# A gated cross-attention and routed-FFN kernel on one core: another order of loading, scaling and splitting the weights at its start

## Chip, cores and metric

The kernel runs on one core of one Trainium2 chip, as one launch. Its time is the device time of that core in microseconds (us). The engines have their own instruction streams: TensorE (PE in the profile, PEld for its weight loads), VectorE (DVE), ScalarE (ACT), GpSimd (POOL) and SyncE (SP), which issues the DMAs here. They are ordered among each other by semaphores alone.

## The reference, cut to what matters

```python
x = x + tanh(g_xattn[0]) * xattn(ctx_1024, layernorm(x), ...)   # x 32x112x256, ctx 32x375x256
x = x + tanh(g_ffn[0])   * routed_ffn(layernorm(x), ...)        # 8 experts, best 2 per token

def xattn(x, latents, ln_m_g, ln_m_b, ln_l_g, ln_l_b, Wq, Wkv, Wout):   # 16 heads of 64
    x, lat = layer_norm(x, ln_m_g, ln_m_b), layer_norm(latents, ln_l_g, ln_l_b)
    q, kv = lat @ Wq, concatenate([x, lat], axis=1) @ Wkv       # Wq 256x1024, Wkv 256x2048
    k, v = split(kv, 2, axis=-1)
    out = softmax(q k^T * 64 ** -0.5) v                         # per head, 112 x 487
    return out @ Wout                                           # Wout 1024x256
```

Inputs and outputs are float32.

## The kernel before, in words

Two parts follow each other: the attention for all 32 batches, and then the routed FFN with its own tiles. Only the first is touched by the change.

**Numbers in two halves.** Each float32 operand of a projection is scaled by a power of two and split into a high and a low float16 half. ScalarE writes the high half (a copy with a scale), and VectorE the low half (scaled operand minus high half, a scalar_tensor_tensor with two inputs in SBUF) for the weights, GpSimd for the normalised inputs (kv_lo, L306). Each product takes three matmuls (`three`, L622): high by high, high by low, low by high.

**Scales.** The power of two comes from the largest magnitude. `weight_scales` (L441) measures five peaks per partition on VectorE (wkv, wq, wout, and two of the layer norms' scales and shifts), TensorE turns them, VectorE takes the maxima, TensorE spreads them over the partitions, and VectorE makes exponents, scales and the factors `undo` that take the scales back. These are one chain for all four scales. `then` (L435) lets VectorE wait for each of its own small steps.

**Steps.** Work on (batch b, pair of heads j) has the step t = 8 b + j. STEPS (L39) runs from t = -24. All engines walk through the same steps, each with its own list. At step t the K and V projections of t + 8 are made (so batch 0's are in steps -8 to -1), the scores of pairs t and t + 1 on even t from t = 0 on, the product with V four steps later. The normalised input of a batch is turned (T, two units of four transposes, at j = 2 and 4, L711), scaled by the layer norm's factors on VectorE (kv_f, L538), and split; Q is made in two units at j = 3 and 7 (L719). The K, V, T and Q units use the two PSUM banks `proj_ps` in turn, and a unit waits until the one before the last has been taken out (`take`, L609): K by k_hi on ScalarE (L401) and k_lo on VectorE (L522), V by L415 and L528, T by L538 and L539, Q by L388 and L513.

**The opening.** SP issues load(0) (context and x of batch 0, L192), wkv in two halves, four small loads of the layer norms' vectors straight into their turned places (L201), tanh's and the gate's, wq, wout, load(1). The float32 weights are staged in the space of v_sb. ScalarE waits for all small loads, makes the tanh, waits for the scales and splits all of wkv (L356), then wq and wout ahead of step -9 (L379, L380). VectorE runs the statistics of batch 0, `weight_scales` at t = -22, the statistics of batch 1, the two kv_f of batch 0, the low half of wkv at t = -11, of wq at t = -6, of wout at t = -2. GpSimd subtracts the means and multiplies by the factors, and makes kv_lo of the first half at j = 4, the subtraction of the next batch at j = 5 and kv_lo of the second half at j = 6. It clears the unused rows of v_sb at t = -9 and t = -1, after the staged weights have been read. TensorE's first K of batch 0 waits for both kv_lo and for wkv's low half (L650 to L652).

## Time and profile before

| | us |
|---|---|
| median of 3 runs | 1881.23 (1879.61 to 1881.39) |
| profiled execution | 1880.83 |
| its span | 1879.1 |
| TensorE busy | 1657.4 (88% of the span) |
| VectorE busy | 1348.8 (72%) |
| ScalarE busy | 1186.2 (63%) |
| GpSimd busy | 1185.2 (63%) |
| DMA | 233.20 MB, mean 124 GB/s |

The span is the time from the first to the last recorded instruction of one execution; the device time holds a little more around it. An engine's busy time is the sum of its instructions; its share of the span is an average over stages with different limits. In a timeline each row is an instruction (or several merged, with their count): start, duration, engine, line, operation, what is written and read, shape, and in brackets how long the engine had been idle before it and what released it.

### The profile page before, as it was taken

How to read it: one execution, taken by the hardware profiler on the slowest of the kernel's cores; microseconds unless marked ns; L12 is line 12 of the kernel's file. 1: busy time of each engine (PE TensorE's matmuls, PEld its weight loads, DVE VectorE, ACT ScalarE, POOL GpSimd, SP SyncE). 2: the span in 40 equal slices, each digit the busy share in tenths (PEclk: the TensorE clock that was granted, in tenths of full speed). 3: DMA queues.
4: the chain of work that ended last, by engine and by line, in shares of the span. 5: the costliest groups of instructions: out<-in, count | busy, mean ns of one | idle time of the engine just before them, and what ended most of it. 6: DMA issues, size and time to landing. Idle time of an engine off the chain costs nothing. (4 is left out here: it accounts for less than half of the span.)

```text
span 1879.1 us, 42970 instructions
## 1 busy us (share of the span) xinstructions
PE 1657.4 (88%) x15031; PEld 1161.6 (62%) x15032; DVE 1348.8 (72%) x3173; ACT 1186.2 (63%) x2666; POOL 1185.2 (63%) x1297
## 2 busy tenths in 40 slices
PE   2899999999999999999999999997303999999980
PEld 0456666666666666666666666665202999989970
DVE  5777877778777787777877778775495666666646
ACT  2587887778877787777877778776244333333320
POOL 4477778777787777877778777767163433434420
PEclk9999999999999999999999999998556999999995
DMA  4267767667777776666766667667454111111119
GB/s 132 50 132 143 152 138 139 138 142 152 138 138 138 142 153 138 136 140 142 154 138 137 139 142 142 129 128 151 124 178 154 51 45 50 47 47 50 45 36 292
DMA packets 599543, 233.20 MB, mean 124 GB/s; under 512 B 534064, under 2 KB 584016, under 8 KB 598992
## 3 DMA queue, kind: packets, MB, share of 16 engines
q1 hardware_dynamic: 592656, 212.67, 52.7%
q0 software_dynamic: 6720, 18.36, 3.2%
q8 instruction: 98, 1.61, 0.3%
q14 instruction: 69, 0.57, 0.1%
HBM read 78.66 MB, written 20.19 MB: 53 GB/s over the span
## 5 line engine op out<-in xcount | busy, mean ns | idle before, releaser
L279 POOL TENSOR_TENSOR p_parts<-p_f,p_parts 112x487 f16<-112x487 f32 x512 | 559.6, 1116 | 185.6 <-ACT p_parts L373 185.6
L364 ACT ACTIVATE p_f<-scores_ps,shift 112x487 f32<-112x487 f32 x512 | 337.7, 664 | 7.9 <-DVE passed L494 4.2
L494 DVE TENSOR_SCALAR_CACHE_REDUCE passed<-scores_ps 112x487 f16<-112x487 f32 x512 | 308.0, 658 | 30.2 <-PE scores_ps L645 30.2
L401 ACT ACTIVATE k_hi<-proj_ps 128x488 fp32r<-128x488 f32 x256 | 148.0, 578 | 256.1 <-PE proj_ps L627 256.0
L1010 ACT ACTIVATE space<-h_ps,b_sb,undo 128x256 f32<-128x256 f32 x280 | 142.6, 559 | 233.4 <-PE h_ps L1239 231.0
L528 DVE SCALAR_TENSOR_TENSOR v_sb<-proj_ps,v_sb 128x512 f16<-128x512 f32 (+1 forms) x256 | 176.9, 691 | 140.6 <-ACT v_sb L415 139.4
L373 ACT ACTIVATE p_parts<-p_f 112x487 f16<-112x487 f32 x512 | 275.8, 607 | 0.0
L522 DVE TENSOR_TENSOR k_lo<-proj_ps,k_hi 128x488 fp32r<-128x488 f32 x256 | 169.0, 660 | 91.4 <-ACT k_hi L401 91.2
L676 PE MATMUL pv_ps<-v_sb,pt_sb 128*128 128x128 f16 x2048 | 218.2, 221 | 7.6 <-DMA pt_sb<-p_parts 4.8
L627 PE MATMUL proj_ps<-kv_hi,wkv_hi 128*128 128x488 f16 x512 | 191.4, 374 | 28.7 <-POOL kv_lo L306 13.5
L627 PE MATMUL proj_ps<-wkv_hi,kv_hi 128*128 128x512 f16 (+1 forms) x512 | 194.3, 379 | 0.3
L627 PE MATMUL proj_ps<-wkv_lo,kv_hi 128*128 128x512 f16 (+1 forms) x512 | 194.1, 379 | 0.0
L627 PE MATMUL proj_ps<-wkv_hi,kv_lo 128*128 128x512 f16 (+1 forms) x512 | 194.0, 379 | 0.0
L627 PE MATMUL proj_ps<-kv_hi,wkv_lo 128*128 128x488 f16 x512 | 189.4, 370 | 0.0
L627 PE MATMUL proj_ps<-kv_lo,wkv_hi 128*128 128x488 f16 x512 | 189.4, 370 | 0.0
L1262 PE MATMUL y_ps<-w_hi,stage 128*128 x1120 | 189.0, 273 | 0.0
L981 POOL DMA_INDIRECT y_rows<-space,y_row_i x70 | 69.4, 991 | 147.7 <-DVE space L1179 137.0
L415 ACT ACTIVATE v_sb<-proj_ps 128x512 f16<-128x512 f32 (+1 forms) x256 | 152.8, 597 | 14.5 <-PE proj_ps L627 5.6
L1239 PE MATMUL h_ps<-xt_hi,w_hi 128*128 128x256 f16 x560 | 154.6, 276 | 5.0 <-DVE xt_lo L1171 5.0
L676 PEld LDWEIGHTS pv_ps<-v_sb,pt_sb 128*128 128x128 f16 x2048 | 134.7, 99 | 37.2 <-DMA pt_sb<-p_parts 5.5
L1239 PE MATMUL h_ps<-xt_hi,w_lo 128*128 128x256 f16 x560 | 154.6, 276 | 0.0
L1239 PE MATMUL h_ps<-xt_lo,w_hi 128*128 128x256 f16 x560 | 154.6, 276 | 0.0
(222 smaller groups left out, 4017.1 us busy)
## 6 DMA issues: line engine op xcount, KB each, us to landing
w_part<-in_L_ffn_w_dram SPq DMA_DIRECT2D x64, 256.0 KB, 3.5
stage<-in_L_ffn_w_dram SPq DMA_DIRECT2D x32, 512.0 KB, 4.5
ctx_sb<-in_ctx_dram SPq DMA_DIRECT2D x32, 375.0 KB
space<-y_rows SPq DMA_DIRECT2D x32, 224.0 KB, 4.7
pt_sb<-p_parts SPq DMA_TRANSPOSE x256, 4.0
x_sb<-in_x_dram SPq DMA_DIRECT2D x32, 112.0 KB
res_sb<-in_x_dram SPq DMA_DIRECT2D x32, 112.0 KB, 5.3
x_dram<-x_sb SPq DMA_DIRECT2D x32, 112.0 KB, 2.9
```

The lines of the kernel that those rows point to most:

```text
L279: pool.tensor_tensor(p_parts[0:LQ, p % PS, h, 1, 0:LK], p_f[0:LQ, p % 2, h, 0:LK], p_parts[0:LQ, p % PS, h, 0, 0:LK], ALU.subtract).then_i ...
L364: act.activation(p_f[0:LQ, p % 2, h, 0:LK], scores_ps[n][0:LQ, 0:LK], ACT.Exp, bias=shift[0:LQ, p // 2 % 2, n:n + 1], scale=-1.0, accum_ou ...
L373: act.activation(p_parts[0:LQ, p % PS, h, 0, 0:LK], p_f[0:LQ, p % 2, h, 0:LK], ACT.Copy).then_inc(p_high, 1)
L401: act.activation(k_hi[:, j], ps[:, 0:LKP], ACT.Copy).then_inc(kq_high, 1)
L415: act.activation(v_sb[0:rows, (b + 1) % 2, c, 8 * half_:8 * half_ + 8, 0], ps[0:rows, :].rearrange("p (n d) -> p n d", d=DH), ACT.Copy, sc ...
L494: dve.tensor_scalar(passed[0:LQ, n], scores_ps[n][0:LQ, 0:LK], P_SHIFT, None, ALU.add, ALU.min, accum_out=shift[0:LQ, p // 2 % 2, n:n + 1] ...
L522: dve.tensor_tensor(k_lo[:, j], ps[:, 0:LKP], k_hi[:, j].bitcast(F32), ALU.subtract).then_inc(kq_low, 1)
L528: dve.scalar_tensor_tensor(out=v_of(1), in0=ps[0:rows, :].rearrange("p (n d) -> p n d", d=DH), scalar=V_SCALE, in1=v_of(0), op0=ALU.mult, ...
L627: last = nc.tensor.matmul(out, lhs(a, k), rhs(c, k), start=(n == 0), stop=(n == 3 * KD - 1))
L676: last = nc.tensor.matmul(pv_ps[:, at:at + 128], block_of(0, c), v_sb[:, sv, c, n].rearrange("p a d -> p (a d)"), start=(c == 0), stop=(c ...
L1239: last = nc.tensor.matmul(h_ps[m][:, c * ROWS:c * ROWS + ROWS], (w1_hi, w1_lo)[a][:, k, bass.ds(e1, 1), f:f + 128].rearrange("p o f -> p ( ...
L1262: last = nc.tensor.matmul(y_ps[s][:, r * D:r * D + D], (g_hi, g_lo)[a][:, s, m, c, r * 128:r * 128 + 128], (w2_hi, w2_lo)[b][:, m * 2 + c, ...
```

## The change

It concerns the opening up to step 1 of the attention.

- The layer norms' four vectors are loaded as rows, two of 128 values each, into `ln_rows`, ahead of load(0), and TensorE turns all eight rows at once into `tail_ps`; VectorE copies them to `affine`.
- wkv is loaded in four chunks of 512 columns (first K, first V, second K, second V), each with its own semaphore. The tanh's and the gate's loads stand behind load(1).
- There are four chains of scales in place of one: for the inputs (turn 0), wkv (1), wq (2), wout (3). wkv is measured chunk by chunk. wq is measured behind wkv's first two low halves and its scale is made at t = -6; wout is measured at t = -4 and its scale made at t = -2.
- The weights are split in seven parts: kv0 and kv1 ahead of the first projection, kv2, q0, kv3, q1 between steps -8 and -3, out at t = -1 (high) and t = 0 (low). TensorE waits for the parts one by one.
- wkv is staged in p_parts and wout in pt_sb; wq stays in v_sb. So v_sb's first half is cleared at the start, and p_parts' and pt_sb's unused columns at t = -1 and t = 1. ScalarE's step 0 waits for p_parts, and the first transpose of p on SP for wout's low half.
- GpSimd makes both kv_lo of batch 0 at j = 4.

```diff
+            for n, a in enumerate((ln_m_g, ln_m_b, ln_l_g, ln_l_b)):
+                sp.dma_start(ln_rows[KD * n:KD * (n + 1), :], a.rearrange("(k p) -> k p", p=128)).then_inc(small_loaded, 16)
             load(0)
-            for k in range(KD):
-                sp.dma_start(stage[:, k], wkv[k * 128:(k + 1) * 128]).then_inc(w_loaded, 16)
-            for n, a in enumerate((ln_m_g, ln_m_b, ln_l_g, ln_l_b)):
-                sp.dma_start(affine[:, n, :], a.rearrange("(k p) -> p k", p=128), allow_slow_non_contiguous=True).then_inc(small_loaded, 16)
-            sp.dma_start(tanh_g[:, :], g_x.partition_broadcast(128)).then_inc(small_loaded, 16)
-            sp.dma_start(gate_sb[:, :, :], gate_w.rearrange("(k p) e -> p k e", p=128)).then_inc(small_loaded, 16)
+            for n in range(4):
+                sp.dma_start(kv_chunk(stage, n), kv_chunk(wkv.rearrange("(k p) n -> p k n", p=128), n)).then_inc(w_loaded[n], 16)
...
             load(1)
+            sp.dma_start(tanh_g[:, :], g_x.partition_broadcast(128)).then_inc(tanh_loaded, 16)
+            sp.dma_start(gate_sb[:, :, :], gate_w.rearrange("(k p) e -> p k e", p=128)).then_inc(gate_loaded, 16)
...
-                if j in (4, 6) and is_batch(nb):
-                    k = (j - 4) // 2
+                halves = ((0, 1) if j == 4 else ()) if nb == 0 else ((j - 4) // 2,) if j in (4, 6) and is_batch(nb) else ()
+                for k in halves:
...
+                if t == -2 * NP + 2:
+                    weight_high("kv0")
+                    weight_high("kv1")
+                if t == -NP - 1:
+                    act.wait_ge(tanh_loaded, 16)
+                    act.activation(tanh_g[:, :], tanh_g[:, :], ACT.Tanh).then_inc(tanh_done, 1)
                 if t == 0:
-                    act.wait_ge(set_up, 2)
+                    act.wait_ge(parts_cleared, PS)
...
+                for turn, at in (("kv2", -8), ("q0", -6), ("kv3", -6), ("q1", -4), ("out", -1)):
+                    if t == at:
+                        weight_high(turn)
...
+            def input_scale():
+                largest(0, 3, 5)
+                power(0, 3, 5)
+                then(dve.tensor_scalar(affine[:, :, :].rearrange("p a k -> p (a k)"), affine[:, :, :].rearrange("p a k -> p (a k)"), scale[:, 3:4], None, ALU.mult))
+
+            def kv_scale():
+                for n in range(4):
+                    dve.wait_ge(w_loaded[n], 16)
+                    last = dve.tensor_reduce(peak_kv[:, n:n + 1], kv_chunk(stage, n), AX.XY, ALU.max, apply_absolute_value=True)
+                then(last)
+                then(dve.tensor_reduce(peak[:, 0:1], peak_kv[:, :], AX.X, ALU.max))
+                dve.sem_inc(peaks_moved, 1)
+                largest(1, 0, 1)
+                power(1, 0, 1)
+                dve.sem_inc(scales_ready, 1)
...
+                if t == -3 * NP:
+                    input_peaks()
                 if t == -3 * NP + 2:
-                    weight_scales()
+                    input_scale()
+                    kv_scale()
                 if t == -NP - 3:
-                    split_kv_weights()
-                if t == -NP + 2:
-                    split_q_weights()
-                if t == -2:
-                    split_out_weights()
+                    weight_low("kv0")
+                    weight_low("kv1")
+                    q_peak()
...
+                for turn, at in (("kv2", -7), ("q0", -5), ("kv3", -5), ("q1", -3), ("out", 0)):
+                    if t == at:
+                        weight_low(turn)
+                if t == -8:
+                    largest(2, 1, 2)
+                if t == -6:
+                    q_scale()
+                if t == -4:
+                    out_peak()
+                if t == -3:
+                    largest(3, 2, 3)
+                if t == -2:
+                    out_scale()
```

On ScalarE and VectorE the parts stand behind the V evacuation of their step (L415, L528), and on VectorE ahead of the T evacuation of the same step. TensorE turns and spreads the peaks of wq behind V at t = -8 and -7, those of wout at t = -3 and -2.

## Rows read from the trace of the kernel before

**Rows 1.** Stretches: bounds, length, busy time of each engine, granted clock, DMA, GB/s.
```profile
40.00:72.00 32.00, 27.13 (x154) 12.69 (x156) 19.01 (x31) 11.14 (x20) 15.35 (x13) 1.00 0.17 48
72.00:86.00 14.00, 12.80 (x71) 6.08 (x68) 11.60 (x33) 10.53 (x25) 5.62 (x7) 1.00 0.18 33
...
200.00:300.00 100.00, 99.07 (x910) 63.97 (x908) 76.87 (x203) 77.98 (x185) 77.33 (x89) 1.00 0.69 138
...
1100.00:1200.00 100.00, 99.07 (x909) 63.87 (x908) 76.48 (x198) 77.34 (x184) 78.05 (x89) 1.00 0.68 133
```

**Rows 2.** TensorE's timeline: the first K and the first V projection.
```profile
40.05 0.59 PE L627 MATMUL proj_ps<-kv_hi,wkv_hi 128*128 128x488 f16 x1 [13.47 <-POOL kv_lo L306]
...
42.46 0.59 PE L627 MATMUL proj_ps<-wkv_hi,kv_hi 128*128 128x512 f16 x1
```

**Rows 3.** SP's timeline: issue of one small load.
```profile
5.15 0.47 SPq L201 DMA_DIRECT2D affine<-in_L_xattn_ln_l_b_dram  x1
```

**Rows 4.** VectorE's timeline up to the low half of wkv.
```profile
7.43 1.08 DVE L546 BATCH_NORM_STATS2 stats<-ctx_sb 125x6 f32<-125x256 f32 x3 [7.29 <-DMA x_sb<-in_x_dram]
...
14.12 4.41 DVE L448 TENSOR_REDUCE att_peak<-v_sb 128x1 f32<-128x4096 f32 x1
...
20.64 2.28 DVE L452 TENSOR_REDUCE att_peak<-v_sb 128x1 f32<-128x2048 f32 x1
23.53 0.28 DVE L455 TENSOR_REDUCE att_peak_t<-tail_ps 5x1 f32<-5x128 f32 x1 [0.61 <-PE tail_ps L605]
...
24.80 0.16 DVE L459 COPY att_peak_e<-tail_ps 128x5 f32<-128x5 f32 x1 [0.73 <-PE tail_ps L607]
...
26.33 0.23 DVE L469 TENSOR_SCALAR affine<-affine,att_scale_i 128x8 f32<-128x8 f32 x1
...
27.89 1.08 DVE L546 BATCH_NORM_STATS2 stats<-ctx_sb 125x6 f32<-125x256 f32 x3
...
29.63 0.64 DVE L538 TENSOR_SCALAR kv_f<-proj_ps,affine 128x375 f32<-128x375 f32 x1
...
31.36 4.60 DVE L481 SCALAR_TENSOR_TENSOR wkv_lo<-v_sb,att_scale_i,wkv_hi 128x2048 f16<-128x2048 f32 x2
```

**Rows 5.** ScalarE's timeline: the high half of wkv.
```profile
26.27 3.89 ACT L356 ACTIVATE wkv_hi<-v_sb,att_scale_i 128x2048 f16<-128x2048 f32 x2 [12.08 <-DVEq L468]
```

**Rows 6.** GpSimd's timeline: kv_lo and the subtraction between its halves.
```profile
31.40 5.53 POOL L306 TENSOR_TENSOR kv_lo<-kv_f,kv_hi 128x488 f16<-128x488 f32 x1
36.89 1.46 POOL L328 TENSOR_TENSOR norm_sb<-ctx_sb,moments 125x768 f32<-125x768 f32 x1
...
38.89 1.10 POOL L306 TENSOR_TENSOR kv_lo<-kv_f,kv_hi 128x488 f16<-128x488 f32 x1
```

**Rows 7.** Timelines of GpSimd and VectorE near 99 us.
```profile
98.61 2.19 POOL L279 TENSOR_TENSOR p_parts<-p_f,p_parts 112x487 f16<-112x487 f32 x2 [1.22 <-ACT p_parts L373]
...
99.34 1.21 DVE L586 TENSOR_REDUCE peaks<-w_part 128x2 f32<-128x1024 f32 x1
```

**Rows 8.** Timelines of TensorE and VectorE: steps -3 and -2, and the first scores.
```profile
60.69 0.38 PE L627 MATMUL proj_ps<-kv_hi,wkv_hi 128*128 128x488 f16 x1 [0.99 <-DVE v_sb L528]
61.94 0.38 PE L627 MATMUL proj_ps<-wkv_hi,kv_hi 128*128 128x512 f16 x1
...
63.47 0.38 PE L627 MATMUL proj_ps<-kv_hi,wkv_hi 128*128 128x488 f16 x1
...
71.72 0.48 PE L645 MATMUL scores_ps<-k_hi,q_hi 64*112 64x488 f32 x2
...
62.74 0.67 DVE L522 TENSOR_TENSOR k_lo<-proj_ps,k_hi 128x488 fp32r<-128x488 f32 x1 [1.24 <-ACT k_hi L401]
64.06 0.69 DVE L528 SCALAR_TENSOR_TENSOR v_sb<-proj_ps,v_sb 128x512 f16<-128x512 f32 x1 [0.65 <-ACT v_sb L415]
64.67 2.34 DVE L489 SCALAR_TENSOR_TENSOR wout_lo<-v_sb,att_scale_i,wout_hi 128x2048 f16<-128x2048 f32 x1
```

**Rows 9.** VectorE's timeline: k_lo of step 1.
```profile
78.54 0.65 DVE L522 TENSOR_TENSOR k_lo<-proj_ps,k_hi 128x488 fp32r<-128x488 f32 x1
```

More of the change, by code:

```diff
@@ L351, in _, with weight_high @@
         def _(act):
-            act.wait_ge(small_loaded, 16 * 6)
-            act.activation(tanh_g[:, :], tanh_g[:, :], ACT.Tanh).then_inc(tanh_done, 1)
-            act.wait_ge(scales_ready, 1)
-            for k in range(KD):
-                act.activation(wkv_hi[:, k], stage[:, k], ACT.Copy, scale=scale[:, 0:1]).then_inc(w_high, 1)
+            def weight_high(turn):
+                if turn == "kv0":
+                    act.wait_ge(scales_ready, 1)
+                if turn == "q0":
+                    act.wait_ge(scales_ready, 2)
+                if turn == "out":
+                    act.wait_ge(scales_ready, 3)
+                    act.activation(wout_hi[:, :, :], stage_out, ACT.Copy, scale=scale[:, 2:3]).then_inc(w_high, 1)
+                elif turn[0] == "q":
+                    n = int(turn[1])
+                    act.activation(q_chunk(wq_hi, n), q_chunk(stage_q, n), ACT.Copy, scale=scale[:, 1:2]).then_inc(w_high, 1)
+                else:
+                    n = int(turn[2])
+                    act.activation(kv_chunk(wkv_hi, n), kv_chunk(stage, n), ACT.Copy, scale=scale[:, 0:1]).then_inc(w_high, 1)
             def exponential(p, h):
@@ L439, in then, with largest @@
                 dve.wait_ge(scale_step, n_step[0])
-            def weight_scales():
-                flat = lambda a: a.rearrange("p k n -> p (k n)")
-                dve.wait_ge(small_loaded, 16 * 6)
-                dve.tensor_reduce(peak[:, 3:4], affine[:, 0:4:2, :], AX.XY, ALU.max, apply_absolute_value=True)
-                dve.tensor_reduce(peak[:, 4:5], affine[:, 1:4:2, :], AX.XY, ALU.max, apply_absolute_value=True)
-                dve.wait_ge(w_loaded, 32)
-                dve.tensor_reduce(peak[:, 0:1], flat(stage), AX.X, ALU.max, apply_absolute_value=True)
+            def largest(turn, first, last):
+                at = slice(first, last)
+                dve.wait_ge(peaks_moved, 4 * turn + 2)
+                then(dve.tensor_reduce(peak_t[0:last - first, :], tail_ps[0:last - first, 0:128], AX.X, ALU.max))
+                then(dve.tensor_scalar(peak_diag[0:last - first, at], ident[0:last - first, 0:last - first], peak_t[0:last - first, :], None, ALU.mult))
+                dve.sem_inc(peaks_moved, 1)
@@ new lines, in power @@
+            def power(turn, first, last):
+                at = slice(first, last)
+                dve.wait_ge(peaks_moved, 4 * turn + 4)
+                then(dve.tensor_copy(peak_e[:, at], tail_ps[:, 128:128 + last - first]))
+                if turn == 0:
+                    then(dve.scalar_tensor_tensor(out=peak_e[:, 3:4], in0=peak_e[:, 3:4], scalar=16.0, in1=peak_e[:, 4:5], op0=ALU.mult, op1=ALU.add))
+                    at = slice(3, 4)
+                then(dve.tensor_scalar(exponent[:, 0, at], peak_e[:, at].bitcast(I32), 23, None, ALU.arith_shift_right))
+                then(dve.tensor_scalar(exponent[:, 1, at], exponent[:, 0, at], -1.0, 268.0, ALU.mult, ALU.add))
+                then(dve.tensor_scalar(exponent[:, 2, at], exponent[:, 1, at], 156.0, None, ALU.min))
+                then(dve.tensor_scalar(exponent[:, 3, at], exponent[:, 2, at], -1.0, 254.0, ALU.mult, ALU.add))
+                then(dve.tensor_scalar(scale_i[:, :, at], exponent[:, 2:4, at], float(2 ** 23), None, ALU.mult))
@@ L468, in weight_scales, with q_scale @@
-                dve.sem_inc(scales_ready, 1)
-                then(dve.tensor_scalar(affine[:, :, :].rearrange("p a k -> p (a k)"), affine[:, :, :].rearrange("p a k -> p (a k)"), scale[:, 3:4], None, ALU.mult))
+            def q_scale():
+                power(2, 1, 2)
                 then(dve.tensor_tensor(undo[:, 2:3], inverse[:, 3:4], inverse[:, 0:1], ALU.mult))
-                then(dve.tensor_scalar(undo[:, 3:4], undo[:, 2:3], inverse[:, 2:3], 1.0 / V_SCALE, ALU.mult, ALU.mult))
                 then(dve.tensor_scalar(undo[:, 4:5], undo[:, 2:3], inverse[:, 3:4], -float(DH) ** -0.5, ALU.mult, ALU.mult))
@@ L473, in weight_scales, with out_peak, out_scale @@
                 then(dve.tensor_scalar(undo[:, 0:1], undo[:, 4:5], inverse[:, 1:2], None, ALU.mult))
+                dve.sem_inc(scales_ready, 1)
+            def out_peak():
+                dve.wait_ge(wout_loaded, 16)
+                then(dve.tensor_reduce(peak[:, 2:3], stage_out, AX.XY, ALU.max, apply_absolute_value=True))
+                dve.sem_inc(peaks_moved, 1)
+            def out_scale():
+                power(3, 2, 3)
+                then(dve.tensor_scalar(undo[:, 3:4], undo[:, 2:3], inverse[:, 2:3], 1.0 / V_SCALE, ALU.mult, ALU.mult))
@@ L683, in _ @@
                     if ob == 0:
-                        pe.wait_ge(w_ready, 4)
+                        pe.wait_ge(w_ready, W_TURN["out"])
                     pe.wait_ge(o_moved[s], 16 * (ob // 2 + 1))
```

120 lines of the change are left out of this document (70 added, 50 removed).

## Prediction

> **What bounds the kernel now.** I read three views in this order. First the stretches of time: from 200 to 300 us TensorE is busy for 99.07 of 100 us, and again so from 1100 to 1200 [rows 1]. So the attention is paced by TensorE, and whatever TensorE has behind it when this regime begins is handed on unchanged to the end; the routed part behind it isn't touched by the change. The opening is different: from 40 to 72 us TensorE is busy 27.13 of 32 us, from 72 to 86 us 12.80 of 14 [rows 1]. Second, TensorE's timeline: the first projection starts at 40.05, after 13.47 us of waiting for GpSimd's kv_lo (L306) [rows 2]. So what the change is worth is (how much earlier the first projection starts) minus (how much longer the eight steps t = -8 to -1 and the first steps behind them take). Third, the timelines of the other engines: up to 40 us for the first term, from 40 to 86 us for the second.
>
> **Loads.** Four row loads now stand ahead of load(0). One such issue costs the SP queue 0.47 us, taken from the smallest scale-and-shift load of before [rows 3], so the first inputs are issued 1.9 us later. The statistics began at 7.43, at once when x had landed [rows 4]; I put them at 9.3. (Bounds: 0, if they land by bandwidth and not by issue, to 2.5.) wkv comes in four chunks behind them; everything else of 4 bytes a piece that stood ahead of wq is gone or behind load(1), so I cost landing at nothing: the reductions begin at 14.1 below, which is when they began before with all of wkv there [rows 4]. The tanh and gate loads go behind load(1); their readers come after t = -9 and later.
>
> **First scales.** Statistics and aggregation take 29.63 - 27.89 = 1.74 [rows 4], so to 11.1. The input scale then runs from largest to the scaled affine: 23.53 to 26.33 + 0.23 = 26.56, that is 3.0 us [rows 4]; its turning on TensorE has been done by then. 14.1. Measuring wkv: 4.41 us for 4096 columns, here in four parts [rows 4], plus 0.1 for the reduction over them: 18.7. From the end of the last peak, 20.64 + 2.28 = 22.92, to the first split on ScalarE, 26.27, passed 3.35 us [rows 4, 5]; one instruction of 0.2 less: 3.2. The scale of wkv is there at 21.9 instead of 26.2. What made before late is plain: it measured wq and wout (two times 2.28 [rows 4]) ahead of all scales, and waited for the smallest loads before it began.
>
> **First halves.** DVE: statistics of batch 1, 1.74, to 23.7; then the two affine halves, 31.36 - 29.63 = 1.73 [rows 4], to 25.4; then only the two wkv chunks that steps -8 to -5 need, 2048 of 4096 columns, half of 4.60 = 2.3 [rows 4], to 27.7. ScalarE has the two high halves (half of 3.89 [rows 5]) at 24.0 and kv_hi at 26.1, so it isn't last. GpSimd: kv_lo stretched to 5.53 while DVE ran its two-input splits and ended 0.97 after them; alone it took 1.10 [rows 6]. I take the same here: first half at 27.7 + 1.0, second at 29.9, because the change lets both go ahead of the subtraction that stood between them (38.89 - 36.89 = 2.0 [rows 6]). q_peak on DVE (2.2 us) now runs beside them; a reduction with one input did not stretch GpSimd: p_parts took 2.19 for two, 1.1 each, across the 1.21 us reduction of w_part [rows 7]. If it did stretch them, 2.2 more. The clearing of v_sb moves to GpSimd's idle time before 9 us and costs nothing. **First projection at 30.0 instead of 40.05: 10 us gained** (bounds 7 to 12).
>
> **The eight steps.** Now the price: what was done before the first projection is put into the steps behind it. A step goes like this [rows 8]: K from 60.69, through ScalarE's k_hi to DVE's k_lo 2.05 later, its bank free 0.73 on: the next K at 63.47, a step of 2.8 us, though TensorE's own work for K and V is 2.5 (K to V 1.25). V from 61.94, v_lo 2.12 later, bank free after 0.75 more. Walking the eight steps of before with these numbers, T and Q units (0.5 and 1.25 us) and its one wq split and one wout split (2.3 each) included, gives the first scores at 71.5; the trace has 71.72 [rows 8]. So the walk is good to some tenths, and DVE has only about 0.6 us free between v_lo and the next k_lo: what is put there and is longer is paid. The same walk of the new order from 30.0, with a quarter-chunk split at 1.14 on DVE and 0.97 on ScalarE (halves of the above):
> - t = -8: ScalarE kv2 high, DVE largest 0.5 (as 24.06 - 23.53 [rows 4], about), then the statistics as before: next K at 34.1, and at 38.0 behind the kv2 split of t = -7.
> - t = -6: DVE power and undo: 24.80 to 26.33 less the one that only the input needs, and three undo steps, together 1.95 us [rows 4], behind v_lo at 41.3, so to 43.9; the T evacuation (0.9) queues behind that, which holds V of t = -5 until 44.9. ScalarE stands at q0 from 41.8 to 43.9, then splits q0 and kv3, 1.9 us, and only at 45.85 takes K of t = -5, which has been ready since 43.5. Behind ScalarE wait k_lo, V's evacuation and everything of DVE.
> - t = -5: Q needs wq_lo 0, which stands on DVE behind k_lo and v_lo: 49.2. TensorE waits 3.0 us there. The next K starts at 50.5.
> - t = -4: out_peak, 2.2 us, stands ahead of the T evacuation; V of t = -3 waits for it until 57.7 (1.9 us idle).
> - t = -3 to -1: q1 split, largest, out scale (1.65 us), wout high (1.9 us on ScalarE): next K's at 59.1 and 62.8, first scores at 67.0.
>
> TensorE idles 10.9 us in these steps, against 6.1 by the same walk of before. They take 37.0 instead of 31.4 by walk: 5.5 longer. **What is left at the first scores: 71.7 - 67.0 - 0.2 for the walk's own lag = 4.5.** A page of the Trainium skill speaks against this stage: TensorE: Matmul & The Clock Gate, section HAM oscillation, says that gaps of idle TensorE can send it back to the half clock. By the rows of this trace I take nothing for it (rival C); by that page the sum could be some us worse.
>
> **The first steps of attention.** The wout split, 2.34 us on DVE [rows 8], moves from t = -2 to t = 0, between v_lo and the statistics. Before, k_lo of t = 1 started at 78.54 with no idle time in front of it [rows 9], and DVE is busy 11.60 of 14 us from 72 to 86 [rows 1]. So all 2.3 of it are late there; DVE's pauses, 14 - 11.60 = 2.4 us in that stretch, about half of them behind the split, take 1.0 back: 1.3 lost (bounds 0 to 2.3). The clearing of p_parts (GpSimd, t = -1, idle then) and the waits of the first transpose and of GpSimd at t = 1 for the wout split cost nothing: by the walk it ends near 75, before ScalarE has turned out the first high half of p.
>
> **Sum.** 10.05 - 5.55 - 1.3 = 3.2 us gained. Against the profiled execution, span 1879.1 and 1880.83 with what lies around it, 1877.6; the median of the three runs, 1881.23, is 0.4 above that execution, so I say 1878.0.
>
> **Rivals.**
> A, the inserted work is hidden. Then the steps are as long as before, 31.7, and 10.05 - 1.3 = 8.8 are gained: 1872.5. For it: TensorE has 5 us idle from 40 to 72 [rows 1]. Against it: that idle time is itself waiting for DVE, and ScalarE's wait at q0 is a new one. 0.12; half of it would do (about 1875).
> B, the beginning gains less. If load(0) lands late by 2.5, q_peak stretches GpSimd (2.2) and the wout split costs its full 2.3, the sum is 10.05 - 0.6 - 2.2 - 5.55 - 2.3 = -0.6: 1881.8. It is decided by where the first projection starts: past 33 us nothing is left. 0.25 that it goes to within 1.5 us of no change.
> C, slower. The first six matmuls of before take 2.41 us, 40.05 to 42.46 [rows 2], those of a later K 1.25, 60.69 to 61.94 [rows 8]: 0.40 and 0.21 apart, as at the lower (1.2 GHz) and the upper (2.4 GHz) level, the former after 13.5 us of idleness, though the granted clock of the stretch is printed as 1.00 [rows 1]. If the 3.0 us of idleness in front of Q at t = -5 bring the lower pace back and it stays, the 48 matmuls of four steps cost 0.2 more each, 9.6, and two Q's 1.2 each, 12 in all, of which the idle 4 us of these steps hide a third: 8 net, 3.2 - 8 = -4.8: 1885.9. The rule of the clock page named above would do this in part; the 4.9 us of short idle times of before brought no such thing by 60.69. The point from which it decides is whether matmuls behind the Q of t = -5 are 0.21 apart. 0.04.
> D, it doesn't do what it says: another late thing sets the first projection (a chunk of wkv, the norm). Each is due 2 us or more ahead by the sum, 0.05, about 1880.
>
> **How the numbers follow.** My forecast has 0.54, with a range of its own from 1876 to 1880. 0.2% of 1881 is 3.8 us, about what a measurement of this kernel can tell from no change. Of the forecast's 0.54 a little under a half, 0.25, lies below 1877.4, and A gives 0.12: faster 0.37. Slower is C and the tail of B: 0.06. The rest, 0.57, is within. The range goes from 1874.5, the half of A, to 1882, the end of B.
>
> **What would show it.** Right: scale of wkv near 22 us, kv_lo's second half ending near 30, first projection right behind; wq split 0 as what ends a TensorE wait of 2 to 3 us in front of Q; out_peak in front of an evacuation, with nearly 2 us idle; first scores near 67; the stretch from 200 us on unchanged. Wrong: kv_lo stretched past DVE's splits by q_peak; stages of half pace; a first projection past 33; or steps no longer than before.

## The result, and the profile after

The changed kernel is slower: 1883.5 us median against 1880.49 for the kernel before in the same comparison, ratio 1.0018 with a 95% interval of 1.0011 to 1.0025, that is 2 to 5 us. The profiled execution has a span of 1882.0 us (1879.1 before). I had said 1878.0, in a range of 1874.5 to 1882.0.

The stretches (bounds, length, busy time of TensorE, its weight loads, VectorE, ScalarE, GpSimd, granted clock, DMA share, GB/s) answer to [rows 1]; first those of the rows, then two short ones for the clock:

```profile
40.00:72.00 32.00, 20.84 (x107) 9.54 (x108) 22.74 (x48) 12.84 (x20) 10.05 (x14) 0.95 0.12 32
72.00:86.00 14.00, 12.51 (x84) 6.43 (x84) 11.87 (x30) 9.96 (x22) 4.38 (x5) 1.00 0.06 11
...
200.00:300.00 100.00, 99.07 (x915) 64.13 (x913) 76.38 (x197) 77.35 (x184) 78.80 (x90) 1.00 0.71 138
1100.00:1200.00 100.00, 99.07 (x913) 64.19 (x912) 76.67 (x200) 77.36 (x184) 78.95 (x90) 1.00 0.68 132
```
```profile
32.00:36.00 4.00, 4.00 (x11) 1.41 (x10) 0.67 (x1) 0.58 (x1) 3.50 (x4) 1.00 0.19 32
60.00:64.00 4.00, 2.77 (x8) 1.03 (x9) 1.54 (x3) 0.61 (x1) 2.68 (x3) 0.59 0.00 0
```

From 200 us on nothing has changed. From 40 to 72 us TensorE does a quarter less, 20.84 us against 27.13, although it began 8.5 us earlier. TensorE's timeline, the lines that answer to [rows 2] and [rows 8] (start, duration, engine, line, operation, tiles, shape, idle time before it and what ended it):

```profile
31.52 0.59 PE L711 MATMUL proj_ps<-kv_hi,wkv_hi 128*128 128x488 f16 x1 [8.46 <-POOL kv_lo L314]
...
36.71 0.44 PE L711 MATMUL proj_ps<-kv_hi,wkv_hi 128*128 128x488 f16 x1
...
47.69 0.42 PE L711 MATMUL proj_ps<-wkv_hi,kv_hi 128*104 128x512 f16 x1 [1.49 <-DVE kv_f L612]
...
52.13 0.22 PE L711 MATMUL proj_ps<-kv_hi,wq_hi 128*128 128x112 f16 x1 [2.95 <-DVE wq_lo L548]
...
61.23 0.61 PE L711 MATMUL proj_ps<-wkv_hi,kv_hi 128*128 128x512 f16 x1 [1.98 <-DVE kv_f L612]
61.63 0.64 PE L711 MATMUL proj_ps<-wkv_lo,kv_hi 128*128 128x512 f16 x1
...
63.98 0.46 PE L711 MATMUL proj_ps<-kv_hi,wkv_hi 128*128 128x488 f16 x1
...
72.02 0.21 PE L711 MATMUL proj_ps<-kv_hi,wq_hi 128*128 128x112 f16 x1 [1.49 <-DVE k_lo L582]
73.31 0.48 PE L729 MATMUL scores_ps<-k_hi,q_hi 64*112 64x488 f32 x2
```

The first projection starts 8.5 us earlier than before, the first scores 1.6 us later: the eight steps take 41.8 us instead of 31.7. The waits are those that the walk had named, with nearly its sizes: 1.49 for V at t = -5, 2.95 for wq_lo at t = -5, 1.98 for V at t = -3, behind out_peak. The 1.49 in front of Q at 72.02 (t = -1) it had not named. The matmuls at 61.23 to 63.98 are 0.4 us apart, the lower pace; the granted clock of 60 to 64 us is 0.59.

The products with V, by tile (count, shortest, median and longest duration in ns, then the starts of the first and the last), of the kernel before and of the changed one:

```profile
L676 PE MATMUL pv_ps<-v_sb,pt_sb x2048: 216/219/314, 92.8 to 1319.0; 128*128 128x128 f16 x187
```
```profile
L770 PE MATMUL pv_ps<-v_sb,pt_sb x2048: 216/219/315, 95.6 to 1320.5; 128*128 128x128 f16 x187
```

The first is 2.8 us later, about what the medians show (3.0). From the first to the last lie 1226.2 and 1224.9 us, so in these two executions the last is only 1.5 later; in all thirteen kernels of this study it is 1224.8 to 1226.2, and what follows up to the end of the span has 558.9 to 561.9 without a pattern. So a single span says nothing below 2 to 3 us here, and I read each kernel by three marks of its opening, with its median and ratio beside them. The marks come from one profiled execution of each kernel. The kernel before was measured anew beside each group of runs, and the ratio is to that: its median was 1880.49 for the changed kernel and e1 to e4, 1879.89 for e5 to e8, 1881.13 for e9 and e10, 1880.48 for e11. So kernels of different groups are better compared by their ratios.

| kernel | first projection | first scores | first product with V | median | ratio to before, 95% interval |
|---|---|---|---|---|---|
| before | 40.05 | 71.72 | 92.8 | 1880.49 | |
| changed | 31.52 | 73.31 | 95.6 | 1883.5 | 1.0018 (1.0011 to 1.0025) |
| e1_apart | 31.63 | 72.92 | 95.2 | 1882.38 | 1.0009 (1.0 to 1.0019) |
| e2_load1_first | 30.06 | 71.77 | 94.1 | 1882.06 | 1.0011 (1.0001 to 1.002) |
| e3_before_halves | 37.90 | 70.67 | 91.8 | 1877.66 | 0.9985 (0.9976 to 0.9995) |
| e4_warm | 31.80 | 71.87 | 94.2 | 1882.24 | 1.0006 (0.9997 to 1.0016) |
| e5_chain_early | 31.49 | 68.74 | 91.0 | 1878.17 | 0.9993 (0.9984 to 1.0003) |
| e7_early_load1_apart | 29.51 | 66.69 | 88.9 | 1876.02 | 0.9977 (0.9968 to 0.9987) |
| e6_all | 29.77 | 65.54 | 87.8 | 1875.6 | 0.9977 (0.9966 to 0.9988) |
| e8_before_halves_warm | 38.29 | 69.83 | 90.9 | 1877.31 | 0.9984 (0.9975 to 0.9994) |
| e9_fill_stage | 31.77 | 73.42 | 95.7 | 1881.64 | 1.0002 (0.9993 to 1.0011) |
| e10_out_earlier | 30.25 | 67.25 | 88.3 | 1875.18 | 0.9967 (0.9955 to 0.998) |
| e11_stats_later | 29.99 | 64.13 | 86.3 | 1872.53 | 0.9958 (0.9945 to 0.9972) |

Two things scatter in these marks that the edits don't explain. The last input of batch 0 landed between 8.98 and 9.71 us in e7, e6, e10 and e11, which have the same loads in the same order, and it moves all that follows. And the number of matmuls at the lower pace differs. I count the K and V matmuls recorded with 0.5 us or more instead of 0.37 to 0.46. In the eight kernels whose first units start without unused matmuls ahead of them, 7 to 14 of them open the eight steps (7 before, 14 in e3, 12 changed, 9 in e1, 7 in e2, 14 in e9, 12 in e5 and e7), and each costs 0.2 us. A difference of 1 us between two kernels can be this alone, and has to be looked for step by step.

### The profile page after: what moved, and what is told of

Same layout as the page of the kernel before. It is cut to its first block and busy times, and to the rows that moved or that the text cites. A ratio compares the mean times of both kernels' runs of the same rounds, so it can differ in the third digit from the quotient of the medians.

```text
span 1882.0 us, 43038 instructions
## 1 busy us (share of the span) xinstructions
PE 1663.0 (88%) x15041; PEld 1163.4 (62%) x15042; DVE 1356.0 (72%) x3205; ACT 1186.7 (63%) x2669; POOL 1179.2 (63%) x1297
```

## The experiments

**Two engines hold each other up.** In the changed kernel the input scale took 1.1 us more than I had given it. VectorE's timeline of the changed kernel:

```profile
12.77 0.15 DVE L488 TENSOR_SCALAR att_exponent<-att_exponent 128x1 int32<-128x1 int32 x1
12.96 1.15 DVE L489 TENSOR_SCALAR att_scale_i<-att_exponent 128x2 int32<-128x2 int32 x1
14.14 0.54 DVE L501 TENSOR_SCALAR affine<-affine,att_scale_i 128x8 f32<-128x8 f32 x1
```

GpSimd's timeline of the same stretch:

```profile
12.61 1.47 POOL L336 TENSOR_TENSOR norm_sb<-ctx_sb,moments 125x768 f32<-125x768 f32 x1
14.04 0.61 POOL L337 TENSOR_TENSOR norm_sb<-x_sb,moments 112x256 f32<-112x256 f32 x1
```

The step of 2 values a partition ends as GpSimd's subtraction does, 14.11 and 14.08; the one of 1 value at 12.77 ran through beside the same subtraction.

> The changed kernel, but GpSimd holds its subtraction for batch 0 back until the input scale is made, and its multiplication for batch 2 until the scale of wout is made. In the changed kernel one VectorE step of 0.17 us took 1.15 (12.96 to 14.11, just as GpSimd's subtraction ended at 14.08), and again 1.34 at 69.22, ending with GpSimd's multiplication at 70.53. Theory: the two engines hold each other up there. Then both steps take 0.17, the affine step 0.23 instead of 0.54, wkv's measuring begins 1.3 earlier (13.4). For the second place the first scores come 1.2 earlier relative to the first projection. Whether the first projection is earlier too is open: if the landing of batch 1's input (23.4) sets its statistics, it stays at 31.5 and the total gains 1.2 us; if not, it starts at 30.2 and the total gains 2.5. Rival: the long steps have another cause (TensorE's or a DMA's), and nothing moves.

```diff
+                    if nb == 2:
+                        pool.wait_ge(scales_ready, 3)
...
+                    if nb == 0:
+                        pool.wait_ge(input_scaled, 1)
...
+                    dve.sem_inc(input_scaled, 1)
```

VectorE's timeline of e1_apart:

```profile
13.00 0.17 DVE L493 TENSOR_SCALAR att_scale_i<-att_exponent 128x2 int32<-128x2 int32 x1
13.20 0.23 DVE L505 TENSOR_SCALAR affine<-affine,att_scale_i 128x8 f32<-128x8 f32 x1
...
23.59 1.08 DVE L624 BATCH_NORM_STATS2 stats<-ctx_sb 125x6 f32<-125x256 f32 x3 [2.34 <-DMA x_sb<-in_x_dram]
```

Both steps are short again, and so is the second place (0.17 at 70.00): the hold-up is shown. The first projection did not move; VectorE waits 2.34 us for batch 1's x in place of 1.10. So of the first hold-up nothing was lost in this kernel, load(1) hid it. From the second I had expected 1.2 us; the first scores come only 0.4 earlier. TensorE's wait in front of Q shrank from 1.49 to 0.90 and the step t = -1 from 5.49 to 4.89 us: half of the 1.2. In front of it two other stretches fell to the lower pace (matmuls 0.4 us apart from 53.12 to 55.9 and from 62.6 to 66.0, 15 in all against 6 in the changed kernel; at the first projection it has 9 of them and not 12). The Trainium skill, SBUF — State Buffer, section SBUF: two separate sides, says that VectorE and GpSimd share one pair of ports, which a GpSimd instruction, or a VectorE one in a two-port mode or (against a GpSimd one that reads SBUF) with two inputs in SBUF, holds for its whole length. The rows agree, the step of two values ending 0.03 us behind GpSimd's instruction; that the step of one value at 12.77 was not held is this trace's own.

**Batch 1's input.**

> The changed kernel with load(1) issued ahead of wq and wout. In the changed kernel VectorE stood idle 1.10 us at 22.4 until x of batch 1 had landed, ahead of the statistics that its queue has in front of kv_f. Theory: this idle time goes, the first projection starts at 30.4 instead of 31.5, and the total gains 1.1 us, all of it kept because the steps behind keep their lengths. Rival: wq or wout now land late (their measuring at 29.4 and 57.7 would wait) or GpSimd is last anyway: no gain.

```diff
+            load(1)
             sp.dma_start(stage_q, wq.rearrange("(k p) n -> p k n", p=128)).then_inc(wq_loaded, 16)
             sp.dma_start(stage_out, wout.rearrange("(j p) n -> p j n", p=128)).then_inc(wout_loaded, 16)
-            load(1)
```

VectorE's timeline, batch 1's statistics, of the changed kernel and of e2_load1_first:

```profile
23.49 1.08 DVE L619 BATCH_NORM_STATS2 stats<-ctx_sb 125x6 f32<-125x256 f32 x3 [1.10 <-DMA x_sb<-in_x_dram]
```
```profile
22.25 1.08 DVE L619 BATCH_NORM_STATS2 stats<-ctx_sb 125x6 f32<-125x256 f32 x3
```

The statistics began without a wait, the first projection at 30.06 and the first scores at 71.77, both 1.5 earlier where the theory had 1.1; batch 0's input had landed 0.26 earlier too. The eight steps keep their length, 41.7 us, but not unit by unit: 7 matmuls at the lower pace at the first projection instead of 12, and 12 later on instead of 6. The interval of the ratio (1.0001 to 1.002) can't tell the total from that of the changed kernel.

**One part of the change alone.**

> The kernel before with one part of the change alone: GpSimd makes both kv_lo of batch 0 at j = 4, ahead of the subtraction for batch 1. Theory: kv_lo's second half ends 2.0 us earlier (38.0), the first projection starts at 38.0 and the first scores at 69.7; the steps behind it stay as they are, so the total is 2.0 us lower than the kernel before. Rival: the subtraction and the clearing of v_sb now come behind and hold batch 1's turned input back by the 2 us: total unchanged.

```diff
-                if j in (4, 6) and is_batch(nb):
-                    k = (j - 4) // 2
+                halves = ((0, 1) if j == 4 else ()) if nb == 0 else ((j - 4) // 2,) if j in (4, 6) and is_batch(nb) else ()
+                for k in halves:
...
                     pool.wait_ge(kvlo_done, 2)
+                    pool.wait_ge(pool_step, subtracted(1))
```

First projection at 37.90, 2.15 earlier; first scores 1.05 and first product with V 1.0 earlier; median 2.8 below before, interval 0.9 to 4.5 us. It is a gain by itself. Half of the 2.15 went in the first steps, where the lower pace lasted longer (14 matmuls and not 7; the second K came 4.98 us behind the first, 3.98 before). The edit put nothing there, so that this half was lost to the scatter, and is not a price of the edit, is likely but not shown.

**The lower pace at the first projection.**

> The changed kernel with 22 unused matmuls of 128x512 (into PSUM that nothing reads then) on TensorE between the first wkv part and the wait for kv_lo, so that TensorE is busy from about 24 us to the first projection. Theory: the first K and V run at the upper pace, 0.21 us apart instead of 0.41 to 0.43 (5.2 us for twelve becomes 2.6), the second K starts 2.3 us earlier relative to the first, and the first scores and the total are some 2 us earlier. Rival: VectorE and ScalarE pace these steps, and the time is given back before the first scores: total unchanged. The unused matmuls may themselves push the first projection back by up to 1 us.

```diff
+                        if b == -1:
+                            pe.wait_ge(w_high, 1)
+                            for i in range(22):
+                                nc.tensor.matmul(tail_ps[:, :], wkv_hi[:, 0, 0:128], wkv_hi[:, 0, 0:512], start=True, stop=True)
                         pe.wait_ge(kvlo_done, 2 * (b + 1) + 2)
```

TensorE's timeline of e4_warm, the unused matmuls:

```profile
23.76 6.39 PE L737 MATMUL tail_ps<-wkv_hi 128*128 128x512 f16 x22 [0.64 <-ACT wkv_hi L376]
```

The second K stands 2.78 us behind the first instead of 5.19: 2.4 us, as expected. At the first scores 1.7 of them are left (40.1 behind the first projection instead of 41.8): K of t = -4 now ran at the lower pace too, beside a stretch at t = -3 and -2 as in the changed kernel. The medians, 1.3 apart, don't tell the two kernels apart.

> The kernel before with GpSimd's two kv_lo of batch 0 behind each other (alone: first projection 37.90, last product with V 2.0 us earlier) and 20 unused matmuls of 128x512 on TensorE from the end of wkv's high half to the first projection. Theory: the first K and V run at the upper pace, the first scores come another 1.5 us earlier (69.1 instead of 70.67), total some 1876. Rival: the steps are paced by VectorE and ScalarE there: total as without them, 1877.7.

In e8_before_halves_warm, which is the run e3_before_halves with 20 such matmuls, the first scores stand 31.5 us behind the first projection instead of 32.8, and come 0.84 earlier. The theory had 1.5, the rival nothing: the second V now waits 1.18 us for VectorE's v_lo, so about half is taken by VectorE. The ratios, 0.9984 and 0.9985, don't tell the two apart.

> The changed kernel with 8 unused matmuls of 128x512 on TensorE in front of the Q unit of t = -5, where it waits 2.95 us, and 8 in front of V of t = -3, where it waits 1.98. In the changed kernel V of t = -3 ran at the lower pace (2.6 us instead of 1.3) behind these waits. Theory: idleness of TensorE brought the lower pace; filled, the V of t = -3 runs at 0.21 us a matmul, no other unit falls, and the first scores come 1.0 to 1.5 us earlier relative to the first projection (from 41.8 us behind it to about 40.5); the total moves by about 1 us. Rival: the fall has nothing to do with idleness, and V of t = -3 or a unit near it is slow as before.

```diff
+                    if t == -3:
+                        for i in range(8):
+                            nc.tensor.matmul(tail_ps[:, :], wkv_hi[:, 0, 0:128], wkv_hi[:, 0, 0:512], start=True, stop=True)
...
+                    if b == -1 and n == 0:
+                        pe.wait_ge(w_high, W_TURN["q0"])
+                        for i in range(8):
+                            nc.tensor.matmul(tail_ps[:, :], wkv_hi[:, 0, 0:128], wkv_hi[:, 0, 0:512], start=True, stop=True)
```

TensorE's timeline of e9_fill_stage, the first matmul of V at t = -5:

```profile
47.92 0.60 PE L711 MATMUL proj_ps<-wkv_hi,kv_hi 128*104 128x512 f16 x1 [1.49 <-DVE kv_f L612]
```

V of t = -3 ran at the upper pace (first matmul 62.36, next K 63.77), and its step took 4.81 us instead of 6.14. But the lower pace had come at 47.9, ahead of the long wait, so it took V at t = -5 and part of the unused matmuls, and the Q unit came 0.9 us later relative to K of t = -5. First scores 41.65 us behind the first projection, as without. That no other unit would fall failed. Up to this V, TensorE's instructions are those of the changed kernel, where the same V, behind the same wait of 1.49, ran at the upper pace (0.42 at 47.69): which unit the lower pace hits is not set by the code alone. The trace is one execution; by the ratios, 1.0002 (0.9993 to 1.0011) against 1.0018 (1.0011 to 1.0025), the kernel is some 3 us below the changed one, with intervals that just touch. So that nothing was gained holds for this trace and is open for the total.

**The place of the work, not its amount.**

> The changed kernel with other places for the work on wq and wout, and the same amount of splitting: both are measured behind wkv's first low halves (VectorE is idle there from 31.6 to 34.8), one chain makes both scales in step -8, and the splits stand one to a step (high kv2 -8, q0 -7, kv3 -6, q1 -5, out -3; low kv2 -7, q0 -6, kv3 -5, q1 -3, out -1). Theory: the places cost, not the work. The waits of TensorE in front of Q at t = -5 (2.95 us), of V at t = -5 and -3 (1.49 and 1.98) and of Q at t = -1 (1.49) go, and with them the second fall to the lower pace (1.3 us for V of t = -3); first projection as before at 31.5, first scores near 66.5 instead of 73.3, the total 6 to 7 us below the changed kernel (about 1877). Rival: VectorE's work between the steps is what costs, wherever it stands (it has some 0.6 us free in a step); then the steps are at most 2 us shorter and the total is 1881 or more.

```diff
                     weight_low("kv1")
                     q_peak()
+                    out_peak()
+                if t == -8:
+                    largest(2, 1, 3)
...
-                for turn, at in (("kv2", -7), ("q0", -5), ("kv3", -5), ("q1", -3), ("out", 0)):
-                    if t == at:
-                        weight_low(turn)
...
                     dve.tensor_scalar(kv_f[:, k, LC:LK], ps[:, LC:LK], affine[:, 2, k:k + 1], affine[:, 3, k:k + 1], ALU.mult, ALU.add).then_inc(kv_affine, 1)
+                for turn, at in (("kv2", -7), ("q0", -6), ("kv3", -5), ("q1", -3), ("out", -1)):
+                    if t == at:
+                        weight_low(turn)
```

ScalarE's list changes with it:

```diff
-                for turn, at in (("kv2", -8), ("q0", -6), ("kv3", -6), ("q1", -4), ("out", -1)):
+                for turn, at in (("kv2", -8), ("q0", -7), ("kv3", -6), ("q1", -5), ("out", -3)):
```

Two things go beyond the places of the splits: VectorE's low halves now stand behind the T evacuation of their step and not ahead of it, and one chain of small steps makes what two made.

TensorE's timeline of e5_chain_early:

```profile
42.89 0.38 PE L705 MATMUL proj_ps<-kv_hi,wkv_hi 128*128 128x488 f16 x1 [2.98 <-DVE k_lo L583]
...
48.70 0.38 PE L705 MATMUL proj_ps<-kv_hi,wkv_hi 128*128 128x488 f16 x1 [1.00 <-DVE v_sb L589]
...
51.57 0.21 PE L705 MATMUL proj_ps<-kv_hi,wq_hi 128*128 128x112 f16 x1 [0.17 <-DVE k_lo L583]
...
68.74 0.48 PE L723 MATMUL scores_ps<-k_hi,q_hi 64*112 64x488 f32 x2
```

From the same first projection the first scores come 4.6 us earlier than in the changed kernel; the wait for wq_lo went from 2.95 to 0.17 and those behind the T evacuations are gone. One new wait took 2.98, for k_lo behind the chain of small steps and the statistics that now stand in step -8, and eight matmuls at the lower pace follow it. So the theory holds for two thirds of its size. The total is 5.3 us below the changed kernel by the medians, 4.7 by the ratios (0.9993 against 1.0018, intervals apart); the rival, 1881 or more, is refuted.

> The kernel of the run above, with load(1) issued ahead of wq and wout, and with GpSimd's subtraction for batch 0 held back until the input scale is made. Each alone, in the changed kernel: load(1) first moved the first projection from 31.52 to 30.06; the subtraction apart moved the scale of wkv 1.1 us forward (VectorE then waited 2.34 us for batch 1's input instead of 1.10) and left the first projection at 31.63. Theory: load(1)'s landing hid the second gain; with both the first projection is at about 29.0, first scores another 2.5 earlier than in the run above, total about 1874.5. Rival: GpSimd's kv_lo or wq's landing takes over and the first projection is at 30 or later.

First projection 29.51, first scores 66.69, 2.0 and 2.05 earlier than in e5_chain_early; the median is 2.2 lower. What e1 couldn't show alone (the early hold-up, hidden by load(1)) shows with e2's edit: the first projection is at 29.51 against 30.06, though batch 0's input landed 0.39 later (8.98 against 8.59). From that landing it is 20.5 us against 21.5: worth 0.9.

> The kernel of the run above with 18 unused matmuls of 128x512 on TensorE ahead of the first projection. In the changed kernel 22 of these brought the first K and V to the upper pace and the first scores 1.7 us nearer to the first projection. Theory: the same here, first scores 1.5 to 2.5 us earlier, total about 1873. Rival: the first steps have VectorE's chain of wq's and wout's scales beside them and are paced by it, so that nothing is gained.

TensorE's timeline of e6_all, between the first K and the first V:

```profile
32.30 0.27 PE L679 MATMUL tail_ps<-ident,att_peak 128*2 128x128 f32 x1 [1.12 <-DVEq L530]
32.41 0.38 PE L708 MATMUL proj_ps<-wkv_hi,kv_hi 128*128 128x512 f16 x1
```

The first scores are 35.8 us behind the first projection instead of 37.2, and come 1.15 earlier; the medians, 0.4 apart, don't tell them apart. Part of what the upper pace gives is taken at once: TensorE is through with the first K sooner and waits 1.12 us for wout's measuring, which VectorE has to do before the first V.

> The kernel with all of it (chains early, load(1) first, subtraction apart, unused matmuls ahead of the first projection; first scores 65.54), with wout's split one step pair earlier: high at t = -5, low at t = -4, and wq's second half high at -4, low at -3. In the kernels so far wout's low half (2.3 us of VectorE) stood at t = 0 or -1, and the first product with V came 22.3 us behind the first scores; where it stood at t = -2 it came 21.1 us behind. Theory: the 1.2 us are this split in the way of the minima; here 21.1 again, first product with V near 87, total about 1 us below 1875.6. Rival: it costs the same at t = -4, where the evacuation of T is queued behind the K and V ones: first scores 1 us later and nothing gained.

Against e6_all:

```diff
-        W_TURN = {"kv0": 1, "kv1": 2, "kv2": 3, "q0": 4, "kv3": 5, "q1": 6, "out": 7}
+        W_TURN = {"kv0": 1, "kv1": 2, "kv2": 3, "q0": 4, "kv3": 5, "out": 6, "q1": 7}
...
-                for turn, at in (("kv2", -8), ("q0", -7), ("kv3", -6), ("q1", -5), ("out", -3)):
+                for turn, at in (("kv2", -8), ("q0", -7), ("kv3", -6), ("out", -5), ("q1", -4)):
...
-                for turn, at in (("kv2", -7), ("q0", -6), ("kv3", -5), ("q1", -3), ("out", -1)):
+                for turn, at in (("kv2", -7), ("q0", -6), ("kv3", -5), ("out", -4), ("q1", -3)):
```

The first product with V is 21.1 us behind the first scores, as predicted, and the first scores 37.0 behind the first projection instead of 35.8: 58.1 against 58.0 in sum. That looks like the rival. But the steps, each from its K to the next (the last to the first scores), say where the 1.2 us are:

| step | -8 | -7 | -6 | -5 | -4 | -3 | -2 | -1 |
|---|---|---|---|---|---|---|---|---|
| e6_all | 4.38 | 5.65 | 5.70 | 5.31 | 4.12 | 2.78 | 3.68 | 4.15 |
| e10_out_earlier | 5.85 | 5.55 | 5.52 | 5.31 | 4.12 | 3.72 | 2.77 | 4.16 |
| e11_stats_later | 5.90 | 3.88 | 4.32 | 5.31 | 4.12 | 3.15 | 3.31 | 4.15 |

TensorE's timeline of e6_all and then of e10_out_earlier, the first K, a matmul of the first V, and the second K:

```profile
29.77 0.38 PE L708 MATMUL proj_ps<-kv_hi,wkv_hi 128*128 128x488 f16 x1 [0.77 <-POOL kv_lo L314]
...
32.63 0.38 PE L708 MATMUL proj_ps<-wkv_lo,kv_hi 128*128 128x512 f16 x1
...
34.15 0.38 PE L708 MATMUL proj_ps<-kv_hi,wkv_hi 128*128 128x488 f16 x1
```
```profile
30.25 0.38 PE L708 MATMUL proj_ps<-kv_hi,wkv_hi 128*128 128x488 f16 x1 [1.68 <-POOL kv_lo L314]
...
33.38 0.63 PE L708 MATMUL proj_ps<-wkv_lo,kv_hi 128*128 128x512 f16 x1
...
36.10 0.38 PE L708 MATMUL proj_ps<-kv_hi,wkv_hi 128*128 128x488 f16 x1
```

The loss is in t = -8, 1.47 us, ahead of everything that the edit moves: the first V ran at the lower pace. Where the split went, t = -3 is 0.94 longer, and t = -2, from which wout's high half has gone (in e6_all ScalarE makes it from 58.17 to 60.16), 0.91 shorter. From the second K on, e10 is 0.2 us shorter up to the first scores and 1.1 in the first steps of attention. So this trace speaks for the theory, not for the rival: the low half at t = -4, with the high half ahead of it, costs nothing net, and the low half at t = 0 or -1 costs 1.2 us. The ratios, 0.9967 and 0.9977, lean the same way and don't separate the two.

> The kernel with all of it (first scores 65.54, first product with V 87.8), with two things taken out of step -8: the statistics of batch 2 (1.3 us of VectorE) go to t = -4, and wout's last factors to t = -7. In the kernels with the early chain TensorE waits 2.9 us for k_lo in front of K of t = -6, behind a chain of small steps and these statistics, and the matmuls right after that wait run at the lower pace (eight of them, 1.7 us). Theory: the wait shrinks to 1.3 us or less, the fall to the lower pace behind it goes, and the price at t = -4 is at most 1 us: first scores 2 us earlier, 63.5, total about 1 us or more below the kernel with all of it. Rival: the lower pace comes anyway (it is not that one wait that brings it), and the statistics cost at t = -4 what they cost at t = -8: first scores within 1 us of 65.5.

```diff
                     q_scale()
+                if t == -7:
                     out_scale()
...
-                if j == 0 and is_batch(nb):
+                if ((j == 0 and nb != 2) or t == -4) and is_batch(nb):
...
-                if j == 1 and is_batch(nb):
+                if ((j == 1 and nb != 2) or t == -4) and is_batch(nb):
```

TensorE's timeline of e11_stats_later:

```profile
43.59 0.52 PE L805 MATMUL proj_ps<-ident,norm_sb 125*128 125x125 f32 x3 [1.01 <-DVE k_lo L586]
...
47.12 0.21 PE L709 MATMUL proj_ps<-kv_hi,wq_hi 128*128 128x112 f16 x1 [0.32 <-DVE k_lo L586]
```

The wait of 2.94 in front of K of t = -6 is gone. The first scores are 34.1 us behind the first projection (35.8 in e6_all) and at 64.13, 1.4 earlier; I had expected 2. The lower pace came another time, for the end of V of t = -8 and K of t = -7, and VectorE's measuring of wout held the first V for 2.20 us. That is 1.5 us in t = -8, ahead of what the edit moves; from the second K to the first scores it is 28.2 us against 31.4 in e6_all. The medians are 3.1 us apart, the ratios 0.9958 and 0.9977. This kernel has the lowest median of the study, and a ratio (0.9945 to 0.9972) clearly below 1; its interval overlaps that of e10.

## Why the prediction was wrong, point by point

**Range and sign.** Forecast 3.2 us faster, measured 3.0 slower. At the first product with V the miss is 95.6 - (92.8 - 3.2) = 6.0 us: 1.5 in the first projection, 4.6 in the eight steps, -0.1 in the first steps of attention.

**First projection, said 30.0, was 31.52.** x landed 0.45 earlier than I had put it (the four row loads took SP 1.3 us and not 1.9). The input scale took 4.1 us instead of 3.0, held up by GpSimd (shown by e1). Then load(1): I gave landings no cost because "the reductions begin at 14.1 below", and looked only at wkv. Batch 1's input stands in front of kv_f in VectorE's queue, is needed 5.5 us earlier than before (at 22.4 instead of 27.9), and its load was still behind wq and wout: 1.10 us (shown by e2). Each transfer that the earlier reader needs had to be looked at, not the first ones. The stretching of kv_lo was right: VectorE's two low halves took 2.4 and both halves of kv_lo ended 2.1 us behind them, 2.2 said. q_peak did not stretch them; VectorE's and then GpSimd's timeline of the changed kernel:

```profile
29.35 2.28 DVE L516 TENSOR_REDUCE att_peak<-v_sb 128x1 f32<-128x2048 f32 x1
```
```profile
27.00 4.46 POOL L314 TENSOR_TENSOR kv_lo<-kv_f,kv_hi 128x488 f16<-128x488 f32 x2
```

GpSimd ends at 31.46 with VectorE's reduction still running to 31.63.

**The eight steps, said 37.0 (37.2 with the walk's lag), were 41.8.** This is the step of the prediction that failed, and the term that turned the sign: the walk put a return of the lower pace at nothing and VectorE's small steps at their length alone. From K to K it was right for t = -7 (3.96 us, 3.9 walked), for t = -6 and -5 together (12.67, 12.5), where the longest wait is, and for t = -2 (3.84, 3.7). What was missing stands in three places.

The first is t = -8: 5.19 us instead of 4.1. At the first K and V the lower pace lasted for twelve matmuls and not for the seven of before. That need not be the change's own, since the number lies between 7 and 14 with either opening, as said above; the walk had taken one execution's number as a fixed one. The second is t = -4 and -3 together: 10.64 us instead of 8.6. A V unit at t = -3 fell to the lower pace again, 1.3 us. That is rival C: its mechanism was there, at a sixth of its price, and one unit long instead of to the end. The other 0.7 I can't put down to one thing. The third is t = -1: 5.49 us instead of 4.2. A step of out_scale was held by GpSimd's multiplication, TensorE waiting 1.49 us behind it; again VectorE's and then GpSimd's timeline:

```profile
69.22 1.34 DVE L489 TENSOR_SCALAR att_scale_i<-att_exponent 128x2 int32<-128x2 int32 x1
```
```profile
69.06 1.47 POOL L319 TENSOR_TENSOR norm_sb<-norm_sb,rstd 125x768 f32<-125x768 f32 x1
```

With the hold-up taken away (e1) the step took 4.89, so 0.6 of its 1.3 is shown to be this, and 0.7 is open. I had read the same hold-up in kv_lo [rows 6] in one direction, GpSimd stretched by VectorE, and not asked what GpSimd does to VectorE. The recorded sum has a gap of its own: 10.9 us idle against 6.1 is 4.8 more, and the steps are 5.6 longer.

That a good part of the price belongs to where the work stands is shown by e5: the same splits in other places, with one chain fewer, took 4.6 of the 10.1 us back. I had also taken "it brought no such thing" from a kernel whose TensorE was idle 4.9 us in 32 as evidence for one that, by my own walk, is idle 11 in 37.

**The first steps, said 1.3, were 1.2.** 22.3 us from first scores to first product with V, 21.1 before. In e10, where the split stands at t = -4, it is 21.1 again: the price is that of the split's place.

**Rivals.** A (the work is hidden) is refuted: the steps are 10.1 us longer. D did in part: load(1) was another late thing. B's sum is nearest, for two reasons it didn't name, and it was bounded at a first projection past 33, while 31.5 was enough for a loss. The range left out cases in which a start near 31.5 meets steps of over 40 us. The lower pace and the steps' price belong together, since each wait makes both; I had put them into separate rivals with 0.25 and 0.04.

**What stays open.** What brings the lower pace within the steps. It appeared in all ten kernels with the new opening, behind waits of 1.1 to 3 us and in other units from kernel to kernel, even with the same instructions up to there (e9, e10); it never came behind the first units of the three kernels with the old opening, where no wait is longer than 1.5. The Trainium skill, TensorE: Matmul & The Clock Gate, section HAM oscillation, ties the half clock to idleness between bursts of matmuls, which agrees with e4, e6 and e8, whose first K ran at the upper pace behind unused matmuls, and with the difference between the openings. e10 shows that these matmuls are no guarantee: its first K ran at the upper pace and its first V at the lower. No run here gives the condition.

## What to carry to other kernels

Starting TensorE earlier is worth only what the stretch behind it doesn't give back: walk the waits of that stretch with the work that was moved into it, and look for a step in which one engine's wait (ScalarE for a scale) is in front of another's inputs. Work that must lie between steps goes where the engine idles anyway (both measurements under the slow first units; with fast first units TensorE waited 1.1 to 2.2 us for the second of them), and a chain made once for two scales costs a step once. Before a difference of 1 us between two traces is put down to an edit, look whether it lies in a stretch that the edit touches. When a reader moves forward, check every load ahead of it in the reader's queue.

## What the runs showed of the hardware that I had not expected

A VectorE step of two values a partition took 1.15 and 1.34 us instead of 0.17 beside a GpSimd instruction with two inputs, to the latter's end, and one of eight values 0.54 instead of 0.23, while the step of one value in front of it took 0.15 beside the same instruction. TensorE's matmuls fell to 0.41 to 0.43 us apart in the midst of the steps, for 4 to 8 matmuls of K and V at a time, with waits of 1.1 to 3 us ahead of them. The granted clock of such a stretch reads 0.59 (60 to 64 us in the changed kernel), while that of the first units, 32 to 36 us, reads 1.00 at the same spacing: for the first units here the spacing tells the pace and the granted clock does not.
